# Decoder layer on one core: four buffers in cross-attention's first steps, keys handled earlier, and the shares behind the first expert slot

## The reference

```
x = x + attn(layernorm(x))          # 16 heads of 16, weights and activations quantised
x = x + xattn(layernorm(x), ctx)    # queries from x, keys and values from ctx (32 x 64 x 128)
x = x + ffn(layernorm(x))           # 8 experts, the best 2 of each token
```

```
q = rmsnorm(h @ Wq, gq);  k = rmsnorm(ctx @ Wk, gk);  v = ctx @ Wv
out = softmax(q k^T / sqrt(128)) v @ Wo
```

## Time and profile before

| | |
|---|---|
| median of three runs | 947.86 us |
| the profiled execution | 947.81 us |
| its span | 945.7 us |
| mean granted TensorE clock | 0.935 |
| PE busy | 787.2 us (83%) |
| DVE busy | 630.3 us (67%) |
| ACT busy | 535.1 us (57%) |
| POOL busy | 381.1 us (40%) |
| cross-attention | some 229 to 613 us |
| first gate matmul of the experts | 670.75 us |

### The profile page before, as it was taken

How to read it: one execution, slowest core, us unless ns; L and a number is a source line. 1 busy time by engine, 2 the same in 40 slices (tenths; PEclk the granted TensorE clock), 3 DMA queues, 4 the chain that set the end, 5 groups by cost and what they waited for, 6 DMA issues and landing times. The chain is left out here.

```text
span 945.7 us, 29408 instructions
## 1 busy us (share of the span) xinstructions
PE 787.2 (83%) x11789; PEld 575.7 (61%) x11789; DVE 630.3 (67%) x1110; ACT 535.1 (57%) x1002; POOL 381.1 (40%) x445
## 2 busy tenths in 40 slices
PE   0599989973887999999999978881699999999992
PEld 0488878851333666566656656661477777777771
DVE  6788999643768999999999888678333333333330
ACT  1688777752656676676767665440254454454450
POOL 0231222231335545555554556300345555555532
PEclk9998999965998999999999989995899999999997
DMA  9110000000454533334433433092682222222223
GB/s 326 44 48 25 26 25 25 25 2 23 126 170 137 151 115 113 114 114 130 139 122 109 136 91 92 2 376 81 238 285 45 40 46 40 41 46 40 40 35 106
DMA packets 59402, 91.97 MB, mean 97 GB/s; under 512 B 6768, under 2 KB 39664, under 8 KB 59088
## 3 DMA queue, kind: packets, MB, share of 16 engines
q1 hardware_dynamic: 48048, 76.26, 24.4%
q0 software_dynamic: 7488, 10.23, 6.7%
q10 hardware_dynamic: 3744, 3.67, 1.1%
HBM read 63.13 MB, written 29.10 MB: 98 GB/s over the span
## 5 line engine op out<-in xcount | busy, mean ns | idle before, releaser
L1549 DVE SCALAR_TENSOR_TENSOR hid<-psu,hid 128x688 f32<-128x688 f32 x39 | 34.1, 875 | 144.6 <-ACT hid L1411 144.6
L1162 PE MATMUL xbank_a<-arena,x_o 128*128 128x256 f16 x768 | 95.9, 275 | 2.6 <-DVE x_sb L1015 1.5
L1411 ACT ACTIVATE hid<-psg 128x688 f32<-128x688 f32 x39 | 29.0, 744 | 117.2 <-PE psu L1624 117.2
L1067 PE MATMUL xbank_qk<-arena 128*128 128x512 f16 x336 | 84.8, 390 | 5.8 <-DVE x_gains L971 3.9
L1162 PEld LDWEIGHTS xbank_a<-arena,x_o 128*128 128x128 f16 x768 | 72.6, 99 | 17.9 <-DVE x_o L986 7.8
L1639 PE MATMUL fbank<-arena,hidT 128*128 (+1 forms) x663 | 82.8, 273 | 0.8 <-ACT f_y L1431 0.8
L1624 PE MATMUL psg<-wgu,f_xT 128*128 x468 | 75.0, 310 | 4.0 <-ACT f_xT L1418 2.2
L1624 PE MATMUL psu<-wgu,f_xT 128*128 x468 | 74.6, 309 | 0.0
L1639 PEld LDWEIGHTS fbank<-arena,hidT 128*128 128x128 f16 (+1 forms) x663 | 63.0, 98 | 15.4 <-issue 9.2
L1385 POOL DMA_INDIRECT token_out<-f_y,f_to x39 | 62.6, 1604 | 17.3 <-issue 16.9
L873 ACT ACTIVATE sqq<-xbank_qk 128x512 f32<-128x512 f32 x56 | 33.4, 596 | 59.7 <-PE xbank_qk L1067 59.7
(11 more groups left out here) (269 smaller groups left out, 2004.7 us busy)
## 6 DMA issues: line engine op xcount, KB each, us to landing
arena<-in_wx SPq DMA_DIRECT2D x51, 256.0 KB, 3.7
wgu<-w_hl SPq DMA_DIRECT2D x8, 1376.0 KB
ao<-key_norms SPq DMA_DIRECT2D x64, 128.0 KB, 3.6
w_hl<-cT SPq DMA_DIRECT2D x26, 256.0 KB, 2.1
w_hl<-x_pair SPq DMA_DIRECT2D x25, 256.0 KB, 3.3
ao<-in_wx SPq DMA_DIRECT2D x16, 256.0 KB, 3.0
w_hl<-ao SPq DMA_DIRECT2D x16, 256.0 KB, 2.1
arena<-w_hl SPq DMA_DIRECT2D x8, 384.0 KB
```

The source lines that it names most:

```text
L1067: last = nc.tensor.matmul(query_bank(h), wq[:, a, k, f:f + D2], hT[:, g, b * NCH + k, :], start=(j == 0), stop=(j == len(terms) - 1))
L1162: last = nc.tensor.matmul(acc[t // 2][:, (t % 2) * C:(t % 2 + 1) * C], o_hl[h % 2][:, a, at:at + P], wvo[:, b, e, :], start=(e == 0 and j ...
L1549: nc.vector.scalar_tensor_tensor(out=h3, in0=psu[:, :].rearrange("p (c n) -> p c n", c=2)[:, :, 0:FH], scalar=HID_UP / (H_UP * W_UP), in1= ...
```

## The change

Three edits.

1. Steps -8 to -3 use four buffers for raw pieces and four for halves. The two new raw buffers are `pf` and `sc[0]`, the two new ones for halves are `o_hl`; all four lie free until step -1. Loads 0 to 3 are issued at once, and save i is followed by load i + 4 up to i = 9. Saves 10 and 11 issue none, and from save 12 on it is load i + 2 as before. There are four semaphores for loads and four for saves.
2. On ScalarE `key(2m)` stands before `turned_copy(N)` and `exponent(n)`, and `key(2m+1)` before `quotient_high(n)`. On VectorE `key_halves(2m)` stands before `sums(n)` and `residual`.
3. `shares()` moves behind slot 0 on TensorE, and VectorE's reading of it behind its part of slot 0. Twenty idle matmuls into `ps[1]` stand where the shares were. TensorE waits for `routed` before it turns the first hidden rows, and ScalarE no longer waits for `shared`.

```diff
         def raw(i):
             r = i % 2
+            if i < early - 4 and i % 4 >= 2:
+                return (pf if r else sc[0])[:, :, :].rearrange("p a s -> p (a s)")
             return (late if i < early else parked)[:, r * PIECE:(r + 1) * PIECE]
+        def loaded_behind(i):
+            if i < early - 6:
+                return i + 4
+            return i + 2 if i >= early - 4 and piece(i + 2) else None
+        def halves_of_before(i):
+            if i < early - 2:
+                return i - 4
+            return i - 2 if not early <= i < early + 2 else -1
         def halves(i):
             r = i % 2
+            if i < early - 4 and i % 4 >= 2:
+                return o_hl[r][:, :, :]
...
                 def piece_save(i):
                     sp.wait_ge(low_odd if i % 2 else low_even, i // 2 + 1)
-                    sp.dma_start(... halves(i)).then_inc(pair_out[i % 2], 16)
-                    if piece(i + 2):
-                        piece_load(i + 2)
+                    sp.dma_start(... halves(i)).then_inc(pair_out[i % 4], 16)
+                    if loaded_behind(i) is not None:
+                        piece_load(loaded_behind(i))
...
-                piece_load(0)
-                piece_load(1)
+                for i in range(4):
+                    piece_load(i)
...
                 def piece_high(i):
-                    act.wait_ge(raw_in[r], (i // 2 + 1) * 16)
-                    if i >= 2:
-                        act.wait_ge(pair_out[r], i // 2 * 16)
+                    act.wait_ge(raw_in[i % 4], (i // 4 + 1) * 16)
+                    before = halves_of_before(i)
+                    if before >= 0:
+                        act.wait_ge(pair_out[before % 4], (before // 4 + 1) * 16)
...
+                    if pair(m):
+                        key(2 * m)
                     if pair(N):
                         turned_copy(N)
                     if pair(n):
                         exponent(n)
-                    if pair(m):
-                        key(2 * m)
                     if pair(N):
                         out_high(2 * N)
                     if pair(m):
                         query(2 * m + 1)
+                    if pair(m):
+                        key(2 * m + 1)
                     if pair(n):
                         quotient_high(n)
-                    if pair(m):
-                        key(2 * m + 1)
...
                     if pair(m):
                         query_low(2 * m)
+                        key_halves(2 * m)
                     if pair(n):
                         sums(n)
                     if N > 0 and N % NU == 0:
                         residual(N // NU - 1)
-                    if pair(m):
-                        key_halves(2 * m)
...
-                act.wait_ge(s["shared"], 1)
                 slot_rounds(act, slot, NSLOT + 1)
...
+                def shares_read():
                     dve.wait_ge(s["shared"], 1)
...
                     if slot_there(n):
                         dve.wait_ge(s["hh_high"], n + 1)
                         nc.vector.tensor_tensor(hid_hl[:, 1, 0:FF], ...)
+                    if isinstance(n, int) and n == 0:
+                        shares_read()
...
-                shares()
+                idle_work(ps[1], 20)
...
                     if slot_there(n, -1):
+                        if isinstance(n, int) and n == 1:
+                            pe.wait_ge(s["routed"], 1)
                         pe.wait_ge(s["hh_low"], n)
...
                 for n in range(-1, NSLOT + 2):
                     slot(n, n % 2)
+                    if n == 0:
+                        shares()
```

More of the change, by code:

```diff
@@ L710, in cross_attention @@
         pair_own = sb("x_pair", [P, 2, PIECE], F16)
-        raw_in, pair_out = [sem(f"x_raw_in{i}") for i in range(2)], [sem(f"x_pair_out{i}") for i in range(2)]
+        raw_in, pair_out = [sem(f"x_raw_in{i}") for i in range(4)], [sem(f"x_pair_out{i}") for i in range(4)]
         high_done, up_done, low_even, low_odd = sem("x_pair_high"), sem("x_piece_up"), sem("x_low_even"), sem("x_low_odd")
@@ L774, in piece_load @@
                         sp.wait_ge(k_done, H2)
-                    sp.dma_start(raw(i), dram["wx"][:, i * PIECE:(i + 1) * PIECE]).then_inc(raw_in[i % 2], 16)
+                    sp.dma_start(raw(i), dram["wx"][:, i * PIECE:(i + 1) * PIECE]).then_inc(raw_in[i % 4], 16)
                 def piece_save(i):
                     sp.wait_ge(low_odd if i % 2 else low_even, i // 2 + 1)
-                    sp.dma_start(dram["w_hl"][:, :, i * PIECE:(i + 1) * PIECE].rearrange("l p n -> p l n"), halves(i)).then_inc(pair_out[i % 2], 16)
-                    if piece(i + 2):
-                        piece_load(i + 2)
+                    sp.dma_start(dram["w_hl"][:, :, i * PIECE:(i + 1) * PIECE].rearrange("l p n -> p l n"), halves(i)).then_inc(pair_out[i % 4], 16)
+                    if loaded_behind(i) is not None:
+                        piece_load(loaded_behind(i))
                 def key_norms_out(b):
@@ L795, in key_norms_in @@
                     if b == 1:
-                        for r in range(2):
-                            sp.wait_ge(pair_out[r], early // 2 * 16)
+                        for r in range(4):
+                            sp.wait_ge(pair_out[r], early // 4 * 16)
                     for u in range(first // 2 + 2 * part, first // 2 + 2 * part + 2):
@@ L814, in _ @@
                             key_norms_in(batch(N - 1 - part), part)
-                for r in range(2):
-                    sp.wait_ge(pair_out[r], (NPIECE + 1 - r) // 2 * 16)
+                for r in range(4):
+                    sp.wait_ge(pair_out[r], (NPIECE + 3 - r) // 4 * 16)
             @block.gpsimd
@@ L1537, in _ @@
                     nc.vector.tensor_tensor(shares_of[:, :, v, :], hits, share[:, v].rearrange("p j t -> p (j t)").unsqueeze(2).to_broadcast([P, NJ, NSLOT]), ALU.mult).then_inc(s["shares_ready"], 1)
-                dve.wait_ge(s["shared"], 1)
-                c.link(nc.vector.tensor_copy(factor[:, :], ps[2][:, 128:128 + NSLOT]))
-                for v in (1, 2):
-                    c.link(nc.vector.tensor_tensor(factor[:, :], ps[2][:, 128 + v * NSLOT:128 + (v + 1) * NSLOT], factor[:, :], ALU.add))
-                c.link(nc.vector.tensor_scalar(factor[:, :], factor[:, :], 1.0 / (HID_UP * W_UP), None, ALU.mult))
-                dve.sem_inc(s["routed"], 1)
+                def shares_read():
+                    dve.wait_ge(s["shared"], 1)
+                    c.link(nc.vector.tensor_copy(factor[:, :], ps[2][:, 128:128 + NSLOT]))
+                    for v in (1, 2):
+                        c.link(nc.vector.tensor_tensor(factor[:, :], ps[2][:, 128 + v * NSLOT:128 + (v + 1) * NSLOT], factor[:, :], ALU.add))
+                    c.link(nc.vector.tensor_scalar(factor[:, :], factor[:, :], 1.0 / (HID_UP * W_UP), None, ALU.mult))
+                    dve.sem_inc(s["routed"], 1)
                 def slot(n, r):
@@ L1560, in _, with idle_work @@
             def _(pe):
-                def idle_work(count):
+                def idle_work(bank, count):
                     for i in range(count):
-                        nc.tensor.matmul(ps[3][:, :], spare_work[:, 0:P], spare_work[:, 0:512], start=True, stop=True)
-                idle_work(32)
+                        nc.tensor.matmul(bank[:, :], spare_work[:, 0:P], spare_work[:, 0:512], start=True, stop=True)
+                idle_work(ps[3], 32)
                 pe.wait_ge(s["wr_in"], 16)
@@ L1577, in _ @@
                         last.then_inc(s["t_done"], 1)
-                        idle_work(2)
+                        idle_work(ps[3], 2)
                     if u:
```

## The result

The changed kernel takes 934.96 us (median of four runs, 934.06 to 935.83) against 947.25 us for the kernel before in the same comparison (946.10 to 951.37). The ratio is 0.9852, 95% interval 0.9830 to 0.9873. The profiled execution took 935.83 us, with a span of 934.0 us and a mean granted clock of 0.939 (before: 947.81, 945.7, 0.935).

A forecast was written before the change was run, and what follows sets the result against it. Bounds taken: first steps by raw-piece DMA waits, ordinary steps by a VectorE-TensorE ring of 10.84 us, then the chain into the first expert slot. 9.3 + 1.2 + 0 + 3.7 = 14.2 us less gives 933.7 us, range 930 to 938.

The forecast's parts named there:

- the pieces: Seven steps ahead of the first scores: four buffers bring 49.18 us to 39.85, 9.3 us won, clock at 1.00.
- the keys: Main stretch of cross-attention: squaring and splitting keys earlier leaves the ordinary step at 10.84 us, effect 0.
- the shares: Ahead of the first expert slot: first gate 4.0 us earlier, 0.3 lost later; 3.7 us won, bounds -0.3 and 4.2.
- The step after: Step behind the seven first ones: its first query no longer at half clock, 1.2 us won, bounds 0 and 1.7.
- The rival of a SyncE queue that holds the loads back: First steps: SyncE's one queue delays loads, or the clock falls; half of 9.3 us stays, 938.4 us; chance 0.09.
- the ring: Ordinary step: VectorE from score product to out_low 7.30 us, hand-over 0.12, TensorE with its hand-over 3.42, together 10.84 us.
- The rival that put 7.5 us on `turned_copy`: Main stretch: the delayed `turned_copy` comes through because 0.2 us of slack is thin; 7.5 us back, 941.2 us; chance 0.14.
- The gathered rows and the idle matmuls: Before the first transposes: idle matmuls end at 665.3 us; gathered rows allow no transpose before 665.2.
- The sums: Share sums behind the second transposes: 1.8 us of work under 1.71 us of cover, 0.3 us lost with issue gap.
- the sentence on SyncE: Behind the first slot: expert 3's load goes some 4 us later, its first user many slots away; no cost priced.

The follow-up runs named there:

- The lighter ring: The changed kernel with VectorE writing only 32 of 512 columns of even pieces' low halves from piece 18 on: 928.58 us (one run).
- ScalarE's half alone: The kernel before with only the even key's square moved ahead of `turned_copy` on ScalarE, VectorE's order as before: 958.28 us (one run).
- the shares alone: The kernel before with only edit 3, `shares()` behind slot 0 and twenty idle matmuls in their place: 947.01 us, ratio 0.9977.
- the load let go earlier: The changed kernel with SyncE's load of expert 3 waiting for the three share products, not VectorE's reading of the sums: 933.02 us, ratio 0.9830.
- the late load: The kernel before with SyncE's load of expert 3 also waiting for the first slot's low half: 950.18 us (one run).
- the keys alone: The kernel before with only edit 2, both reorderings on ScalarE and VectorE: 946.71 us, ratio 0.9986.

## Why the prediction was right, and where it was wrong

The forecast was 933.7 us, and 934.96 was measured: 14.2 us forecast, 12.3 found. The mechanism of the large part was right. That the sum came so near is in part luck: by the traces the pieces gave 10.5 us, as forecast, the keys 1.7 to 1.9 more than the nothing forecast, and the shares lost about 1 where 3.7 were to be won.

**Pieces: right in kind and size.** Forecast 39.85 us for the seven steps, measured 39.67; the clock is 1.00 through them, and the waits at the raw pieces are gone except for pieces 14 and 15, as named. The step after was put at 1.2 us won and gave 1.6, and the next gave another 0.33 that the sum did not have. With the four buffers alone the two take 9.53 and 10.89 us: 1.2 won, exactly as forecast, and 0.1 lost. The other 0.4 us in each come with the reordering of the keys. The rival of a SyncE queue that holds the loads back has nothing left to explain.

**Keys: the ring held.** The period is 10.80 us, inside the 10.8 to 10.9 named, although the largest single wait of TensorE in that stretch, 12.8 us, was removed. The term was 0 and is 1 to 2 us: the hand-over from out_low to the projection, named as 0.12, shrank to 0.06 us, where TensorE now waits for out_low (0.18 us in the step shown), and the two steps after the first scores gave 0.9. `turned_copy` is late for `attend` as forecast (0.17 us of wait in the step shown, 5.5 us over the stretch). Attend starts 3.93 us behind the score product, where it was 3.69: 0.24 us later, forecast 0.25. It is paid out of the key's former wait. The lighter ring, 10.45 us, and ScalarE's half alone, 11.15 us with a run longer by 0.30, show from both sides that VectorE's run between score product and out_low set the period. The rival that put 7.5 us on `turned_copy` did not come; a cost of that size does come when only half of the edit is made, by another path, VectorE's sums.

**Shares: the front right, the rear wrong.** The first gate was forecast 4.0 us nearer to the names and came 4.15 nearer. The gathered rows and the idle matmuls were nearly level, as the bounds had it: TensorE waits 0.65 us for the rows behind the idle matmuls, and those took 5.83 us, not 6.2. The prediction takes the low clock at 659 us from the earlier trace rows, which show it at 664.3; the trace has the same 0.50 at 659. The sums were to stick out by 0.3 us and stick out by nothing. The Trainium skill's 81 ns per matmul (page TensorE: Matmul & The Clock Gate, section Back-to-back issue gap) would have put 2.6 us there, an estimate. The measured 1.89 us by the order in time agree with the row used instead.

The step that failed is the sentence on SyncE: "SyncE's load of expert 3 waits for that reading and goes some 4 us later; its first user is many slots away." Both halves are true as such, and the load went 8 us later measured from the first gate. The cost was sought at the load's user, and it lay with the load's neighbours: the scatters and gathers of GpSimd. Part three was 3.7 us in the sum, bounds -0.3 and 4.2, and by the trace it lost about 1 in the full change (4.15 won at the first gate, 5.1 given back) and 0.7 alone, below its bounds. The stall is shown to come with this part (the shares alone), to change its place when the load is moved (the load let go earlier), and to vanish when the load is spread over slots (930.97 us). With it gone, slots 0 to 9 take 56.64 us, and the third part gives the 3.7 us and a little more.

Open: why scatters and gathers beside the same full load take 7 us in one kernel and 8 or more in another, so that a load that starts late with the shares in their old place leaves GpSimd's waits at 4 us, and not 5 to 6. The time from the load's start to the first scatter does not order them: 10.9 us in the changed kernel (wait 5.26), 11.7 with the late load (4.17), 19.2 in the kernel before (3.88), 21.4 with the early load (6.56). No run varied one thing alone.

## What to carry to other kernels

Find the ring that sets a period, from one engine's instruction through hand-overs back to itself one period later, before pricing a wait: the largest wait can lie beside it, and removing it then wins only the hand-over. When an edit moves the start of a bulk load, price the small transfers that will run beside it, not only the load's user; where these stand in one engine's fixed order with single buffers, give the load out in pieces tied to the consumer's progress. An experiment on a kernel that still has a stall behind the place it changes can show nothing, because the stall gives back what was lost or takes what was won.

## What the runs showed of the hardware that I had not expected

- A scatter of 128 result rows by GpSimd takes 8.38 us to land and a gather 7.93 us while the expert loads move 386 to 394 GB/s. In the kernel before a scatter beside 385 GB/s took some 7 us, and 7.29 beside 392 GB/s with the late load, so that rate alone does not say how long it takes. With one load group a slot, GpSimd's wait for the scatter is 0.72 to 0.85 us, against 5.26 and 6.07.
- Keeping one expert's load in flight instead of several leaves the scatter's wait at 5.27 and 5.69 us, though only 290 GB/s were moved during the first of the two scatters.
- TensorE fell to its lower level (1.2 GHz) in the stall: seventeen down matmuls took 3.40 us behind an idle time of 3.38 us, where they take 1.96 at the upper level. So about 1.4 of the 5.1 us of the stall are clock.
- The kernels with four buffers seem to vary less from run to run: 936.1 to 937.6 us and 932.6 to 933.6 in four runs each, where the kernel before went from 943.5 to 952.8 in 23 beside them. Where the variation lies is not shown: the seven first steps took 49.18 us in the trace of an execution of 947.81 us and 48.79 in one of 952.27 (the keys alone).
